# A mixture-of-experts block: the second layer's loop over row halves turned outward, and rows of the last norm set between the links of two chains

## The reference

```
x = x + layernorm(attention_sum(layernorm(x)))      # row sums of exp(q k), then a tiny two-layer net
x = x + layernorm(moe(layernorm(x)))                # 8 experts, each row goes to 2 of them

logits = flat @ gate_w + gate_b;  topv, topi = top_k(logits, 2);  topw = softmax(topv)
for each expert e:
    h = gelu(flat @ w1[e] + b1[e])                  # 256 -> 1024
    out = h @ w2[e] + b2[e]                         # 1024 -> 256
    acc = acc + out * routing_weight[:, e]
```

## Time and profile before

| | |
|---|---|
| median of 3 runs | 688.99 us (685.15 to 689.6) |
| profiled execution, its own time | 692.22 us |
| its span, first to last instruction | 690.4 us |
| mean granted TensorE clock | 0.909 |
| TensorE busy | 562.9 us, 82% of the span |
| VectorE busy | 425.9 us, 62% |
| ScalarE busy | 366.7 us, 53% |
| GpSimd busy | 184.4 us, 27% |
| layer one and layer two of the 34 tiles in the chain that ended last | 23% and 24% of the span |

### The profile page before, as it was taken

How to read it: one execution, slowest core, us unless ns; L and a number is a source line. 1 busy time by engine, 2 the same in 40 slices (tenths; PEclk the granted TensorE clock), 3 DMA queues, 4 the chain that set the end, 5 groups by cost and what they waited for, 6 DMA issues and landing times.

```text
span 690.4 us, 14876 instructions
## 1 busy us (share of the span) xinstructions
PE 562.9 (82%) x4170; PEld 507.8 (74%) x4175; DVE 425.9 (62%) x1446; ACT 366.7 (53%) x821; POOL 184.4 (27%) x153
## 2 busy tenths in 40 slices
PE   2768756766855798999999999989989999999920
PEld 1536344344345598999999999989989999999910
DVE  4958764936885675555545556558567754454547
ACT  3364632734733544464646456667569554553651
POOL 2000071071072266232322222312213231312210
PEclk9958977967977989999999999999999999999975
DMA  8910020091021176332323235355365232322567
GB/s 226 381 35 0 1 100 23 0 334 48 1 100 40 65 180 210 56 46 46 46 46 46 46 46 170 48 153 168 46 167 159 40 55 38 54 38 47 163 154 245
DMA packets 51848, 66.73 MB, mean 97 GB/s; under 512 B 4870, under 2 KB 45292, under 8 KB 51692
## 3 DMA queue, kind: packets, MB, share of 16 engines
q1 hardware_dynamic: 37804, 47.87, 22.0%
q0 software_dynamic: 14016, 18.56, 15.7%
HBM read 38.26 MB, written 28.74 MB: 97 GB/s over the span
## 4 chain that ended last, share of the span: by engine, by line
PE 61%; DVE 11%; ACT 9%; issue 7%; another core or an unknown queue 7%; DMA 3%; DVEq 1%; ACTq 0%; POOLq 0%; POOL 0%
PE pY L1527 24%; PE pL L1515 23%; PE pP L722 3%; DMA sum_y<-y,dest 2%; PE pP L823 2%; PE pS L739 2%; PE pX L439 2%; DVE z L1652 2%; ACT xn L569 1%; ACT z L1666 1%; PE pT L707 1%; ACT xrow L636 1%; PE pS L788 1%; ACT h L1450 1%
## 5 line engine op out<-in xcount | busy, mean ns | idle before, releaser
L1450 ACT ACTIVATE h<-pL,b_now 128x256 f32<-128x256 f32 x272 | 112.3, 464 | 152.5 <-PE pL L1515 146.0
L517 POOL DMA_INDIRECT sum_y<-y,dest x70 | 113.6, 1623 | 286.0 <-DVE y L1571 261.0
L1527 PE MATMUL pY<-w_hi,h_lo 128*128 128x256 f32 x544 | 154.9, 285 | 4.8 <-DVE h_lo L1544 4.5
L1515 PE MATMUL pL<-xeT_hi,w_lo 128*128 128x256 f32 x544 | 151.7, 279 | 6.3 <-issue 5.7
L1527 PE MATMUL pY<-w_hi,h_hi 128*128 128x256 f32 x544 | 151.7, 279 | 0.0
L1527 PE MATMUL pY<-w_lo,h_hi 128*128 128x256 f32 x544 | 151.5, 279 | 0.0
L1515 PE MATMUL pL<-xeT_lo,w_hi 128*128 128x256 f32 x544 | 151.1, 278 | 0.0
L1515 PE MATMUL pL<-xeT_hi,w_hi 128*128 128x256 f32 x544 | 150.9, 277 | 0.0
L1544 DVE TENSOR_TENSOR h_lo<-h,h_hi 128x512 fp32r<-128x512 f32 x136 | 92.8, 691 | 93.6 <-ACT h_hi L1456 92.6
L1515 PEld LDWEIGHTS pL<-xeT_hi,w_lo 128*128 128x128 f32 x544 | 102.0, 187 | 7.6 <-issue 6.9
L1527 PEld LDWEIGHTS pY<-w_hi,h_lo 128*128 128x128 f32 x544 | 102.9, 189 | 6.0 <-DVE h_lo L1544 5.4
(11 more groups left out here) (266 smaller groups left out, 844.5 us busy)
## 6 DMA issues: line engine op xcount, KB each, us to landing
w_stage<-w SPq DMA_DIRECT2D x16, 1024.0 KB
xt<-sorted_x SPq DMA_DIRECT2D x38, 260.0 KB
sum_y<-fill SPq DMA_DIRECT2D x1, 4352.0 KB, 19.6
w_stage<-sum_y SPq DMA_DIRECT2D x8, 512.0 KB, 7.8
out<-z SPq DMA_DIRECT2D x8, 512.0 KB, 3.0
x_all<-x SPq DMA_DIRECT2D x3, 1024.0 KB, 8.3
sorted_x<-fill SPq DMA_DIRECT2D x8, 260.0 KB
sum_y<-y,dest POOLq DMA_INDIRECT x70
```

The costliest lines, as they stand in the source:

```text
L517: pool.indirect_dma_start(out=sum_y, out_offset=bass.IndirectOffsetOnAxis(ap=to[:, i:i + 1], axis=0), in_=rows[:, i, :], in_offset=None, c ...
L1450: a = act.activation(h[:, c, :], pL[:, bk, i * TM:(i + 1) * TM], ACT.Gelu, bias=b1_now[par][:, c:c + 1])
L1515: mm = pe.matmul(pL[:, bk, i * TM:(i + 1) * TM], w[:, 0, col], x[:, k, :], start=(k == 0 and w is lo), stop=(k == KC - 1 and x is xeT_lo))
L1527: mm = pe.matmul(pY[:, i, 0:D], s[:, c, rows], w[:, 1, c * D:(c + 1) * D], start=(c == 0 and s is h_lo), stop=(c == FC - 1 and w is lo))
```

## The change

In TensorE's tile the two loops of layer two change places: all 8 chunks for the tile's first 128 rows, then all 8 for the others. The waits for h_split stand in the first of the two passes only. The matmuls, their operands and the number of semaphore raises stay; l2_done for the first half now comes after 24 matmuls, and not after 45.

In the last norm the second and third chain begin before the rows of the group ahead are all written: 5 of the 12 rows of the first group stand alone, and 7 stand behind a link of the second chain each; 9 of the second group stand alone and 3 stand behind links of the third. A row is issued right after a link's operation, ahead of the next wait for out_link. (Chain itself is unchanged. rsqrt calls the chain object for each of its ten operations.)

```diff
@@ tensor: tile
-                for c in range(FC):
-                    if c % 2 == 0:
-                        pe.wait_ge(h_split, 4 * g + c // 2 + 1 + ONE)
-                    for i in range(TM // P):
-                        rows = slice(i * P, (i + 1) * P)
+                for i in range(TM // P):
+                    rows = slice(i * P, (i + 1) * P)
+                    for c in range(FC):
+                        if i == 0 and c % 2 == 0:
+                            pe.wait_ge(h_split, 4 * g + c // 2 + 1 + ONE)
                         for s, w in ((h_lo, hi), (h_hi, hi), (h_hi, lo)):
@@ vector: last norm
-                def apply(v):
...
-                for v in range(len(GROUPS)):
-                    root(v)
-                    apply(v)
+                def row(t):
+                    s, u = t // SG, t % SG
+                    done = dve.scalar_tensor_tensor(out=z[s][:, u, :], in0=y_sum[s][:, u, :],
+                                                    scalar=frstd[:, t:t + 1], in1=x_all[:, t, :],
+                                                    op0=ALU.mult, op1=ALU.add)
+                    if u == SG - 1:
+                        done.then_inc(out_ready, 1)
+                class RowsBetween(Chain):
...
+                    def __call__(self, ins, own=False):
+                        self.n += 1
+                        ins.then_inc(self.sem, 1)
+                        if self.first < self.end_row:
+                            row(self.first)
+                            self.first += 1
+                        self.eng.wait_ge(self.sem, self.done * self.links + self.n)
...
+                begin = [SG * s0 for s0, s1 in GROUPS] + [TT]
+                root(0)
+                for v, alone in ((1, 5), (2, 9)):
+                    for t in range(begin[v - 1], begin[v - 1] + alone):
+                        row(t)
+                    root_beside(v, begin[v - 1] + alone, begin[v])
+                for t in range(begin[-2], TT):
+                    row(t)
```

More of the change, by code:

```diff
@@ new lines, in _, with rows @@
+                class RowsBetween(Chain):
+                    def rows(self, first, end):
+                        self.first, self.end_row = first, end
+                        return self
+                    def __call__(self, ins, own=False):
[5 more added lines that the diff above has]
+                        self.eng.wait_ge(self.sem, self.done * self.links + self.n)
@@ new lines, in root_beside @@
+                def root_beside(v, first, end):
+                    s0, s1 = GROUPS[v]
+                    part = slice(s0 * SG, s1 * SG)
+                    ch = RowsBetween(dve, out_link, v, OUT_LINKS).rows(first, end)
+                    dve.wait_ge(act_squared, s1 * SG)
+                    ch(dve.tensor_scalar(fsum[:, part], fsum[:, part], 1.0 / D, None, ALU.mult))
+                    rsqrt(ch, frstd[:, part], fsum[:, part], [fwork[:, i, part] for i in range(3)])
+                    ch.end()
```

## The result

| | before | after |
|---|---|---|
| median | 689.24 us (685.15 to 689.6, 4 runs) | 702.22 us (701.03 to 703.94, 4 runs) |
| ratio, 95% interval | | 1.019 [1.0163, 1.0217] |
| profiled execution (span) | 692.22 us (690.4) | 701.27 us (699.5) |

The changed kernel is 13 us slower; 697.6 was forecast, within 690.5 to 703.0.

A forecast was written before the change was run, and what follows sets the result against it. TensorE was taken to bound the loop, so each added wait is paid in full. Loop +11.1, tail -1.5 and last norm -1.0 us sum to +8.6, carried to the median: 697.6 us, range 690.5 to 703.

The forecast's parts named there:

- tiles 2 to 13, 24 to 28: Second layer of 17 plain tiles: TensorE waits 0.20 us for bank 3 plus 0.09 us restart in each, +4.9 us.
- tiles 14, 18: First tiles of experts, bank 3 split later: wait of some 1.0 us plus 0.1 restart each, +2.2 us together.
- tiles 22, 23: Tile 22's wait for bank 3 is taken up by tile 23's existing 1.98 us stand for VectorE: 0.
- tiles 17, 21: VectorE leaves the tile before sooner, second layer starts up to 1 us sooner; banks 2 and 3 wait 0.9: -0.2 us.
- tiles 0, 1: Loop's start: 18 more matmuls behind tile 1's bank 3, 14 at the 1.2 GHz level; +3.8 us, ends 2.0 and 4.5.
- tail: After the loop: tile 32's second scatter can go 1.8 us sooner, so VectorE's wait for y_left shrinks; -1.5 us.
- last norm: Ten rows behind chain links make pairs of 0.48 to 0.52 us, not 0.603; -1.0 us, ends -1.3 and +0.5.
- Theory C: Later theory, tile 1: ScalarE's stall ends 8.7 to 11 us after VectorE takes tile 0's rows, whatever TensorE's order.
- (d): Last norm: pairs as slow as link and row together, 698.6 us; chance 0.62 together with the forecast.
- (a): Loop and tail: waits cheaper at 6.4 us, tail gives -3; about +3.4, 692.4 us; chance 0.27.
- (b): Faster: tile 32's y_left wait of 3.82 us goes, capped at 2.6; with other gains about -6 us; chance 0.08.
- (c): Loop: short waits make TensorE's clock swing to 1.2 GHz for 14 matmuls a tile, 45 us, 734; chance 0.03.

The follow-up runs named there:

- bank3_earlier: The changed kernel with the first half's banks in the order 0, 1, 3, 2, so bank 3 is needed 6 matmuls sooner: 723.16 us, ratio 1.0515 to before.
- late_hand: The changed kernel, but VectorE takes the first half's rows only when both halves are done: 704.36 us, ratio 1.0217 to before.
- before_again: The kernel before, unchanged, run again for a second profile: 687.74 us, ratio 1.0006.
- norm_only: The kernel before with only the last norm changed, second layer old: 687.27 us, ratio 0.9981 to before.
- rest_old: The changed kernel with the old second-layer order in all tiles but those run by function first (0, 14, 17, 18, 21 to 24, 32): 691.65 us, ratio 1.0046.
- first_old: The changed kernel with the old second-layer order in the tiles run by function first (0, 14, 17, 18, 21 to 24, 32): 691.7 us, ratio 1.0061.
- l2_only: The kernel before with only the second layer's loops turned, last norm old: 701.57 us, ratio 1.0182 to before.
- after_again: The changed kernel, unchanged, run again for a second profile: 698.75 us, ratio 1.0147 to before.
- before_third: The kernel before, unchanged, run once more for a third profile: 688.54 us.
- rest_old_again: The kernel of rest_old a second time, on a faster chip: 657.14 us beside 655.69 us of the kernel before there, ratio 1.0008.
- mix36_norm: The kernel before with the new norm and a mixed second-layer order that needs bank 3 after 30 matmuls: 686.90 us, ratio 0.9969 to before.

## Why the prediction was right, and where it was off

By its own terms, in us, "measured" being the mean of the two profiles of the changed kernel less the mean of the three of before:

| term | predicted | measured |
|---|---|---|
| tiles 2 to 13, 24 to 28 | +4.9 | +4.8 |
| tiles 14, 18 | +2.2 | +2.1 |
| tiles 22, 23 | 0 | +0.7 |
| tiles 17, 21 | -0.2 | -0.5 |
| eight others | +0.4 | +0.8 |
| tile 33 | left out | +0.3 |
| tiles 0, 1 | +3.8 | +5.4 |
| tail | -1.5 | -1.5 |
| last norm | -1.0 | -1.3 |
| sum | +8.6 | +10.8 |

**The bound** was read rightly: TensorE had no slack in plain tiles, so each wait was paid in full. Of the forecast 0.29 us 0.31 + 0.22 - 2 x 0.1133 = 0.30 us stand in the records. Against the clean 11.34 us the tiles are 0.32 longer, and bank3_earlier confirms both the need and the restart. In the table the 17 tiles measure +4.8 and not +5.4 only because some of before's own ran at the slower spacing described below.

**Tiles 14 and 18**: 11.85 and 11.74 became 12.85 and 12.69 in the first pair, as worked out. **Tile 22's wait** was to be taken up by tile 23's stand of 1.98 us. It was, in the first pair (25.65, 25.79), but that stand is not a fixed thing: the pair took 25.65, 25.32 and 24.31 us in the three profiles of before. One execution had been taken for all. **Tiles 17 and 21**: direction and mechanism right (late_hand: 0.9 each if it is taken away), a little undersized.

**Tiles 0 and 1** are the term that failed. The step was "18 more matmuls behind bank 3, and the 1.2 GHz level for 14 matmuls again". It held ScalarE's progress fixed and moved only TensorE. In fact the stall, in which ScalarE waits for something that the trace calls remote, caught it with fewer of tile 1's banks done. Read from the timelines:

| | banks done at the stall | stall's end, us after tile 0's start | tile 1's end, us after the stall's |
|---|---|---|---|
| before | 3 | 24.3 | 3.8 |
| before_again | 3 | 22.4 | 4.7 |
| norm_only | 3 | 23.9 | 3.8 |
| rest_old | 3 | 25.4 | 3.8 |
| first_old | 3 | 22.9 | 5.8 |
| after | 1 | 22.2 | 10.1 |
| l2_only | 1 | 21.9 | 10.2 |
| late_hand | 2 | 23.6 | 10.2 |
| after_again | 2 | 22.4 | 11.4 |

In before_third all four were done, and the trace has no remote wait there. ScalarE's rows at the end of the stall, of first_old and of rest_old:

```profile
271.12 0.84 ACT L1450 ACTIVATE h<-pL,b_now 128x256 f32<-128x256 f32 x2 [5.05 <-remote]
...
273.45 0.84 ACT L1450 ACTIVATE h<-pL,b_now 128x256 f32<-128x256 f32 x2 [5.02 <-remote]
```

The 18 matmuls came as forecast where three banks were done: 5.8 us in first_old against 3.8 in before, norm_only and rest_old. Behind the wait for bank 3, 13 and 14 matmuls came at a spacing of 0.21 us in after and l2_only, as forecast too, but 25 and 27 in after_again and late_hand. rest_old has no such stretch in tile 1. What the forecast lacked is the banks left behind the stall, one spacing of 1.39 us for each (after's splits end at 276.13, 277.52 and 278.91). Against that, in the first pair the stall ended 2.1 us sooner after tile 0's start in the changed kernel.

What fixes the stall's place I can't settle. It ended 7.9 to 11.0 us behind the time at which VectorE took up tile 0's rows; a tile 0 that ends 1.2 us later moves tile 1's banks towards it. But rest_old has that later tile 0 and still had three banks done. Theory C thus stays argued, not shown. Nor is the stall the whole price of these tiles: before_third has none among tile 1's banks and took 27.8 us, against 25.0 in rest_old_again; VectorE's first split of tile 1 ended 9.2 us after the tile's start in the one and 3.9 us in the other.

**The tail** was right in sum and by its parts: the second scatter followed its rows by 0.78 us and was issued 3.68 us ahead of tile 33's second layer, not 2.04 (1.64 us sooner, 1.8 forecast). rest_old, which turns tile 32, has the same 3.68, and first_old, which doesn't, 2.04. The norm's start lay 4.29 us behind the last y in all profiles, whichever norm followed, as VectorE's own instruction stream would have it; that this stream is the cause is not shown. In the changed kernel ScalarE's squares were still running at 677.87, and the profile still names them as releaser: the name was a coincidence both times.

**The norm**: pairs of 0.47 us instead of 0.603 in ten places give 1.3, the lower end I had named. So the term's rival (d) fell. The Trainium skill, "VectorE: DVE Perf Modes", section "The DRAIN you can't avoid", would have had the pairs save nothing by its sentence that a semaphore costs nothing extra; the same section also says that a next operation that is not held starts earlier, and that is what the runs show. Here the wait of a link on the one before costs 0.13 us beyond the spacing of independent operations (0.206 and 0.08), and a row put into it makes that good.

**Rivals.** (a) fell: the restart after a wait is real and not a model's artefact (0.22 us behind every waiting matmul, and whole tiles longer by it), and tiles 0 and 1 cost more, not less. (b) fell with it: y_left's wait shrank by 1.4 us, not 3.8. (c) fell: the granted clock stayed 1.00 over the twelve plain tiles of the window above with a stand in each, and likewise in bank3_earlier with stands of some 0.7 us. The depth-cycling that the Trainium skill describes in "TensorE: Matmul & The Clock Gate", section "A second HAM failure mode: psum-queue depth-cycling", did not set in here; the case it tells of is another, in bf16 with 512 columns.

The sum of terms, +10.8, lies below both differences of the medians, 13.0 and 11.5 us. Of the forecast's 4.6 us too little 2.2 are in the terms, most of it tiles 0 and 1. The rest no term explains; it is of the size by which executions differ: tile 0 began at 251.6, 248.0 and 249.5 us in the three profiles of before, and at 251.7 and 248.5 in the two of the changed kernel.

## What to carry to other kernels

Before an inner loop is turned, write down for each operand when it is needed and when it is ready, from one tile of the timeline: 0.2 us at one place in a back-to-back loop is paid once per tile, with the restart's 0.1 on top, and the waits view may not list it. A turned loop that needs early what is made late can be mixed: keep the early hand-over of the first half's result and place the late operand's first use past its arrival, as mix36_norm does (it lost nothing; a gain of the order itself is not shown). Put independent work behind each link of a chain of small dependent operations; take terms that rest on one long stall from several profiles, not from one.

## What was not expected of the hardware

- **A chip without the stalls.** On one chip both kernels ran in 655.7 and 657.1 us and not in 688 to 692. The one profile from that chip, rest_old_again, has none of ScalarE's "remote" waits (29 to 45 us in the thirteen other profiles) and the same plain tiles of 11.34 us. The cause isn't known from these runs; the kernel before was timed there but not profiled.
- **Two spacings at full clock.** Layer one of tile 12 in before runs 48 matmuls from 393.09 to 398.42 us, 0.1133 apart; tile 15's from 429.20 to 434.74, 0.1178 apart. The granted clock reads 1.00 for both. The spacing changed only at seams: between tiles, between the two layers of a tile (before's tile 20, to the faster one), or at a wait within layer two (after's tile 19, to the slower one). Tiles 0, 14, 17, 21, 23 and 29, each the first of an expert, began at the slower one in all five profiles of the two kernels; tile 22, also a first one, never did. Layer one ran at the slower spacing in 14 or 15 tiles of before and in 8 or 9 of the changed kernel. What selects it is open.
- **A restart costs one more matmul spacing.** The second matmul starts 0.20 us after the first at the start of a plain tile's layer two, and 0.22 us after it behind a wait in the middle of that layer, where 0.113 us is the spacing otherwise.
